# Two half-chunks of the shared expert done in the tail, one diagonal block per pair weighted by GpSimd, and a new instruction order

## The reference

```
xn  = layernorm(x)
q,k,v,gate = xn @ w_attn            # 16 query heads, 8 kv heads, head size 64
log_G = cumsum(log_sigmoid(6.9 + gate))
s   = rope(q) . rope(k) / 8
a   = exp(2*log|s| + log_G[t] - log_G[s] - max), causal       # = s^2 * decay, scaled
y   = (a @ v) / (sum(a) + 1e-6);  y = normalise(y) * ln_w
x1  = y @ w_proj
h   = layernorm(xn)*g + b
routed = top-2 of 7 experts, capacity 366 tokens, silu(h@W1)*(h@W3) @ W2, gated
shared = silu(h @ W1s) * (h @ W3s) @ W2s
out = x + x1 + routed + shared
```

## Time and profile before

| what | value |
|---|---|
| runs of the kernel before | 1078.84, 1072.55, 1076.85 us (median 1076.85) |
| profiled execution: its own time | 1071.44 us |
| profiled execution: span from first to last instruction | 1069.7 us |
| mean granted TensorE clock | 0.953 of full speed |
| PE busy | 941.8 us (88%) |
| DVE busy | 810.0 us (76%) |
| ACT busy | 682.6 us (64%) |
| POOL busy | 600.6 us (56%) |

### The profile page before, as it was taken

The page is one execution under the profiler, slowest core; times in us unless marked ns, Lnnn a source line. Parts: engine busy times, 40 slices in busy tenths (PEclk is TensorE's granted clock), DMA queues, the critical chain, the costliest instruction groups (busy, mean ns, idle before and its releaser), DMA issues.

```text
span 1069.7 us, 22031 instructions
## 1 busy us (share of the span) xinstructions
PE 941.8 (88%) x8487; PEld 661.7 (62%) x8487; DVE 810.0 (76%) x1503; ACT 682.6 (64%) x1141; POOL 600.6 (56%) x520
## 2 busy tenths in 40 slices
PE   4999989979898989999897989898998989898962
PEld 2675566656565756566665666665766666666642
DVE  5678648878888897778795868688777879686962
ACT  2343458767576767677586677677667768678730
POOL 0311429677767787655565574747366556556441
PEclk9999999999999999989998989899998999999985
DMA  9301213252525252614434342634252443434137
GB/s 264 88 1 45 55 47 90 64 114 49 125 50 124 48 124 73 133 46 99 109 72 97 76 99 67 142 68 107 72 132 55 102 107 77 103 80 94 42 56 197
DMA packets 92792, 96.00 MB, mean 90 GB/s; under 512 B 26605, under 2 KB 77677, under 8 KB 92560
## 3 DMA queue, kind: packets, MB, share of 16 engines
q1 hardware_dynamic: 87616, 91.92, 36.3%
q0 software_dynamic: 5072, 2.67, 1.8%
HBM read 49.47 MB, written 14.50 MB: 60 GB/s over the span
## 4 chain that ended last, share of the span: by engine, by line
PE 49%; DMA 17%; ACT 11%; DVE 9%; SPq 8%; issue 3%; POOL 1%; POOLq 0%; ACTq 0%; DVEq 0%
PE PS L570 15%; PE PS L748 12%; PE PS L778 9%; DMA Kt<-Kt 7%; DMA U<-H_d 6%; ACT U L924 6%; SPq L448 3%; SPq L499 3%; PE PS L613 2%; PE PS L616 2%; PE PS L623 2%; DMA SQ<-R_d 2%; ACT U L850 2%; ACT AX L924 1%; DVE PS L1349 1%
## 5 line engine op out<-in xcount | busy, mean ns | idle before, releaser
L748 PE MATMUL PS<-Qt,Kt 64*128 64x256 f32 (+1 forms) x2560 | 318.0, 394 | 64.7 <-DMA Kt<-Kt 36.6
L748 PEld LDWEIGHTS PS<-Qt,Kt 64*128 64x128 f32 x2560 | 251.3, 204 | 124.2 <-issue 36.8
L924 ACT ACTIVATE U<-PS,ESG,ES 128x512 f32<-128x512 f32 x288 | 206.7, 790 | 128.0 <-PE PS L748 116.7
L778 PE MATMUL PS<-U 128*64 128x256 f32 (+1 forms) x1920 | 202.2, 358 | 8.2 <-POOL U L1473 4.5
L778 PEld LDWEIGHTS PS<-U 128*64 128x64 f32 x1920 | 133.2, 137 | 77.9 <-issue 9.6
L1462 POOL TENSOR_TENSOR U<-U,consts 128x512 f32<-128x512 f32 x96 | 124.4, 1296 | 91.0 <-DMA U<-U 90.3
L1343 DVE TENSOR_TENSOR PS<-U 128x512 f32<-128x512 f32 x64 | 74.6, 1165 | 66.6 <-POOL U L1473 56.6
L1479 POOL TENSOR_SCALAR_AFFINE_SELECT U<-U 128x256 f32<-128x256 f32 x128 | 53.4, 420 | 113.2 <-ACT U L850 112.6
L1473 POOL TENSOR_TENSOR U<-U 128x768 f32<-128x768 f32 x41 | 76.2, 1858 | 61.6 <-ACT U L913 61.5
L1523 POOL TENSOR_TENSOR U<-U,SQ 128x1024 f32<-128x1024 f32 x32 | 77.8, 2430 | 54.6 <-DMA SQ<-R_d 54.6
L1349 DVE TENSOR_TENSOR PS<-U,PS 128x512 f32<-128x512 f32 x144 | 99.8, 693 | 7.6
(11 more groups left out here) (181 smaller groups left out, 1456.7 us busy)
## 6 DMA issues: line engine op xcount, KB each, us to landing
U<-U SPq DMA_DIRECT2D x192, 128.0 KB
U<-H_d SPq DMA_DIRECT2D x32, 512.0 KB
SQ<-R_d SPq DMA_DIRECT2D x64, 256.0 KB, 7.3
Kt<-Kt SPq DMA_DIRECT2D x32, 256.0 KB
U<-in_w SPq DMA_DIRECT2D x21, 256.0 KB, 4.8
acc<-in_x SPq DMA_DIRECT2D x4, 512.0 KB, 5.4
ye_d<-SQ SPq DMA_DIRECT2D x4, 512.0 KB, 7.4
R_d<-U SPq DMA_DIRECT2D x16, 128.0 KB
```

What stands on the lines that cost most here:

```text
L748: mm = te.matmul(bank[:, 256 * n:256 * n + 256 - lo], Kt[u % 2][(ki + hd) % 2][rows, 128 * j:128 * j + 128], Qt[p % 2][m // 2][rows, 256 * ...
L778: mm = te.matmul(P[4][64 * hd:64 * hd + 64, c + lo:c + 256], vt, A[s % NA][:, o:o + 256 - lo], start=begins and n == 0, stop=ends and n == 1)
L924: sq = s.activation(A[n % NA].rearrange("p (a n t) -> p n a t", a=2, n=2)[:, t], PS[:, first:first + 1024].rearrange("p (a n t) -> p n a t ...
```

## The change

`NTAIL = 2`: of the 8 halves of the shared expert `NSH = 6` stay in the opening. Halves 6 and 7 are transposed and used by the router there as before, but their `h` is kept in its own place (`HX`), and their up steps (`sup`, 16 single products), silu, product, down (`sdn`) and addition are new jobs of pair 31. Their weights are loaded once more (`sload`, three DMAs of 256 KB) into tiles of the raw queries, after the last swap. `HEAVY` is (3,) for all pairs, so in 23 pairs VectorE weights the w=1 block. All order tables have new numbers. ScalarE's off-diagonal squares wait for both scalings of ES (v_es 2 in place of 1). The work area grows by 256 columns.

```diff
+NTAIL = 2
+NSH = 8 - NTAIL
-HEAVY = [(3,)] * 9 + [(1, 3)] * 23
+HEAVY = [(3,)] * 32
...
-PE_FIRST: ("up", 33.04, 24.16, 6.2, 8, 4), ("down", 66.9, 24.8, 6.12, 8, 2)
+PE_FIRST: ('up', 33.34, 24.43, 6.57, 6, 4), ('down', 68.18, 25.67, 3.14, 6, 2)
-ACT_FIRST: ("silu", 39.95, 23.79, 6.11, 8, 4), ("es", 169, ...), ("e1", 172.32, ...), ("q", 190.18, 4, ...)
+ACT_FIRST: ('silu', 42.27, 24.01, 5.66, 6, 4), ('es', 181.22, ...), ('e1', 184.04, ...), ('q', 174.79, 1.88, ...)
-POOL_FIRST: ("scatter", 170.28, 4.09, 0, EARLY, 1), ("select", 294.1, 6.18, 0, 2, 1), ("q", 232.63, 8.35, 0, 2, 1)
+POOL_FIRST: ('scatter', 228.56, 15.63, 0, 6, 1), ('select', 263.31, 3.96, 10.48, 2, 1), ('q', 228.76, 11.76, 12.28, 2, 1)
...
+PE_AT: (19.99, 'sup', 0), (20.54, 'sup', 1), ... (28.15, 'sup', 8), (30.4, 'sup', 9), ... (41.42, 'sup', 15), (39.13, 'sdn', 0), (51.12, 'sdn', 1)
+ACT_AT: (19.39, 'sup', 0), (24.8, 'sup', 1), (25.33, 'sup', 2), (31.2, 'sup', 3), ... (64.65, 'sup', 7)
-ACT_AT: (35.85, 'sq', 0), (28.66, 'sq', 1), (62.53, 'down', 0), (15.77, 'square', 5)
+ACT_AT: (36.29, 'sq', 0), (30.5, 'sq', 1), (60.94, 'down', 0), (17.71, 'square', 5)
-POOL_AT: (9.49, 'heavy', 3), (69.16, 'norm', 0), (55.0, 'norm', 1)
+POOL_AT: (8.43, 'heavy', 3), (69.05, 'norm', 0), (61.0, 'norm', 1)
-SP_AT: (26.0, 'tops', 0), (33.34, 'rows', 0), (34.86, 'roots', 0), (36.65, 'spread', 0)
+SP_AT: (-11.68, 'sload', 0), (4.85, 'tops', 0), (26.83, 'rows', 0), (36.3, 'roots', 0), (37.69, 'spread', 0)
...
+                elif kind == "sload":
+                    sp.wait_ge(s_sq, 64 * 32)
+                    sp.wait_ge(g_q, 64)
+                    sy.dma_start(TW[0], w1s).then_inc(s_tw, 16)
...
-                ac.wait_ge(p_sd, 8)
-                ac.wait_ge(p_cb, 32)
+                ac.wait_ge(p_sd, NSH)
+                ac.wait_ge(p_cb, 4 * NSH)
...
@@ TensorE @@
+                elif kind == "sup":
+                    c, n = divmod(job[2], 8)
+                    f, w = divmod(n, 2)
+                    pb = bank_of(job)
+                    pe.wait_ge(s_tw, 48)
+                    te.matmul(pb[:, :], TW[w][:, 128 * f:128 * f + 128], HX[c], start=True, stop=True).then_inc(p_su, 1)
@@ TensorE @@
+                elif kind == "sdn":
+                    for q in range(4):
+                        for f in range(4):
+                            pe.wait_ge(v_su, 4 * c + f + 1)
+                            mm = te.matmul(pb[:, 128 * q:128 * q + 128], TG[c][f][:, 128 * q:128 * q + 128],
+                                           TW[2][:, 128 * f:128 * f + 128], start=f == 0, stop=f == 3)
...
@@ ScalarE @@
+                elif kind == "sup":
+                    s.activation(TG[c][f], P[BANK["sup", 31, 8 * c + 2 * f]][:, :], ACT.Silu).then_inc(a_su, 1)
...
@@ VectorE @@
+                elif kind == "sup":
+                    v.tensor_tensor(TG[c][f], TG[c][f], P[BANK["sup", 31, 8 * c + 2 * f + 1]][:, :], ALU.mult).then_inc(v_su, 1)
@@ VectorE @@
+                elif kind == "sdn":
+                    v.tensor_tensor(acc[:, o:o + 512], P[BANK[job]][:, :], acc[:, o:o + 512], ALU.add).then_inc(v_add, 1)
```

More of the change, by code:

```diff
@@ L55 @@
[L55 to L58, removed]
@@ new lines @@
+POOL_FIRST = [('norm', 79.34, 39.6, 7.36, 3, 1), ('scatter', 228.56, 15.63, 0, 6, 1), ('select', 263.31, 3.96, 10.48, 2, 1), ('k', 165.65, 16.94, 4.66, 2, 1), ('q', 228.76, 11.76, 12.28, 2, 1)]
+PE_AT = [(19.99, 'sup', 0), (20.54, 'sup', 1), (20.7, 'sup', 2), (20.8, 'sup', 3), (20.9, 'sup', 4), (21.0, 'sup', 5), (21.1, 'sup', 6), (21.81, 'sup', 7), (28.15, 'sup', 8), (30.4, 'sup', 9), (30.5, 'sup', 10), (30.95, 'sup', 11), (31.64, 'sup', 12), (31.69, 'sup', 13), (34.43, 'sup', 14), (41.42, 'sup', 15), (39.13, 'sdn', 0), (51.12, 'sdn', 1), (35.76, 'ss', 0), (68.82, 'wp', 0), (68.9, 'wp', 1), (3.61, 'xe', 0), (10.73, 'up', 0), (14.29, 'up', 1), (17.1, 'up', 2), (34.37, 'up', 3), (38.24, 'up', 4), (39.12, 'up', 5), (45.06, 'up', 6), (48.07, 'up', 7), (50.63, 'down', 0), (-26.21, 'k', 0), (-26.07, 'k', 1), (-18.13, 'q', 0), (-17.97, 'q', 1), (-13.58, 'v', 0), (6.96, 'v', 1)]
@@ L64 @@
 SP_FIRST = [("row", 0), ("swapk", 0), ("swapq", 0), ("keys", 0)]
-SP_AT = [(26.0, 'tops', 0), (33.34, 'rows', 0), (-26.51, 'swapk', 0), (-25.12, 'swapq', 0), (-21.73, 'keys', 0), (-21.74, 'row', 0), (-10.42, 'weights', 0), (-6.32, 'weights', 1), (34.86, 'roots', 0), (36.65, 'spread', 0)]
+SP_AT = [(-11.68, 'sload', 0), (4.85, 'tops', 0), (26.83, 'rows', 0), (-32.78, 'swapk', 0), (-23.64, 'swapq', 0), (-21.41, 'keys', 0), (-22.29, 'row', 0), (-21.4, 'weights', 0), (-11.64, 'weights', 1), (36.3, 'roots', 0), (37.69, 'spread', 0)]
 LOAD_AT = [20 * EXPERT_PAIRS[-1] + 76 + b for b in range(B)]
@@ L122, in wanted @@
         return p % 2 == i
+    if kind in ("sload", "sup", "sdn"):
+        return p == 31
     if kind in ("xe", "up", "down", "weights", "combine"):
@@ L254, in block_program @@
         SWPk = take(1024)
-        take = carve(6912)
+        take = carve(7168)
         Vt = [take(1024) for _ in range(2)]
@@ L261, in block_program @@
         ZT, RT, RR, MF = (take(256) for _ in range(4))
-        take = carve(20224)
+        take = carve(20480)
         HR = take(1024)
-        EXPERTS = 21248
+        EXPERTS = 21504
         take = carve(EXPERTS)
@@ L273, in block_program @@
         HL = sb("HL", 1)
+        HX = [U[:, 6144 + 512 * i:6656 + 512 * i] for i in range(NTAIL)]
+        TW = [U[:, 512 * i:512 * i + 512] for i in range(3)]
+        TG = [[RAWk[:, 0:512], RAWk[:, 512:1024], SWPk[:, 0:512], SWPk[:, 512:1024]],
+              [Kt[0][i][:, 512 * j:512 * j + 512] for i in range(2) for j in range(2)]]
         take = carve(3072)
@@ L286, in block_program, with hidden @@
         wv_ = take(512)
+        def hidden(half):
+            return HX[half - NSH] if half >= NSH else hT[:, 512 * half:512 * half + 512]
         hn_v = hn.rearrange("p (k c) -> p k c", c=HS)
@@ L348, in read_out @@
                 return v_wp, 2 * i + job[2] + 1
+            if kind == "sup":
+                n = job[2]
+                return (a_su, n // 2 + 1) if n % 2 == 0 else (v_su, n // 2 + 1)
+            if kind == "sdn":
+                return v_add, NSH + job[2] + 1
             if kind == "xe":
@@ L1121, in forget @@
                 v.tensor_scalar(ESG[:, :], ES[:, :], GUARD, None, ALU.mult).then_inc(v_es, 1)
-                chain(v.tensor_scalar(ES[:, :], ES[:, :], 0.125, None, ALU.mult))
+                v.tensor_scalar(ES[:, :], ES[:, :], 0.125, None, ALU.mult).then_inc(v_es, 1)
                 yield
```

77 lines of the change are left out of this document (49 added, 28 removed), and 7 rows, old and new, of tables (ACT_FIRST, PE_FIRST).

## The result

| | before | after |
|---|---|---|
| median of the runs | 1074.7 us (1068.89 to 1078.84, 4 runs) | 1044.33 us (1036.64 to 1050.26, 4 runs) |
| profiled execution: own time, span | 1071.44, 1069.7 us | 1044.84, 1043.0 us |
| mean granted TensorE clock | 0.953 | 0.982 |
| first scores | 142.30 | 126.66 |
| loop, first scores to the end of the last values | 884.8 us | 871.2 us |

The ratio is 0.972 (95% interval 0.964 to 0.980): 2.8% faster, some 30 us. I had forecast 1062, 15 us faster.

The account below looks back on a forecast made before the run. TensorE was taken to bound the opening and pair loop, a chain of small steps the tail. Start -18, loop 0, tail +3 made -15: 1056.4 profiled, 1062 us as median; range 1048 to 1074, likeliest case 1054 to 1069.

Parts of the forecast that it names:

- Part 1, the start: Opening: two shared-expert halves leave, scores start at 125.2, limited by GpSimd's query rotation; 18 us gained, between 11 and 25.
- the upper bound: First scores: ScalarE's exponential table load now lies before them; 1 us gained, bounds 0 and 2.3.
- Part 2, the loop: Pair loop: TensorE bounds it, so moved weighting and new order change nothing at the end; 0, with 8 us either way.
- my own sign: Failure test: first scores later than 131, or loop from first score to last value over 10 us from 885.
- HEAVY at zero: Loop: the w=1 block of 23 pairs goes from GpSimd to VectorE; 0 at the end, 2 us of slack for 1.
- The loop gains as well: Rival: a fifth of the loop's some 65 us of TensorE idle goes, 13 us, total 1049; chance 0.15.
- square behind sq: Rival: each odd pair's last ScalarE square comes late in 16 pairs, with a slower clock after; 1084 us; chance 0.1.
- Part 3, the tail: After the last values: added expert work delays the chain, partly won back; +3 us, bounds +0.5 and +11.
- The up products that I feared at the lower clock: Rival, tail: 8 ups cost 13.8 instead of 6.9 us and wp 6.3; 8 us more, total 1070; chance 0.2.
- the 2.5 us for less DMA beside it: Tail: new SP order issues loads earlier, so about 0.5 MB less competes with the spread; 2.5 us back.
- the 0.6 assumed: Tail: last wp gets 0.6 of 1.3 us back, with TensorE at work until a few us before.
- Carrying over: From profiled execution to median: the 5.4 us by which the shown runs' median exceeded it was added, 1056.4 to 1061.8.

Follow-up runs that it names:

- e11: The changed kernel with first queries rotated before all scatters, four VectorE operations before the routing wait, eight useless tail products: 1043.03 us, 0.970 of before.
- e4: The kernel before with three useless TensorE products ahead of the first score of each even pair from pair 2 on: 1061.82 us, ratio 0.987.
- e9: The kernel before with only ScalarE's sq of the even pair moved ahead of the odd pair's last off-diagonal square: 1068.24 us, ratio 0.995.
- e13: The kernel before with only HEAVY = (3,) in all pairs, so VectorE weights the w=1 block in 23 pairs: 1074.56 us, ratio 1.001.
- e8: The kernel before with GpSimd's new order list alone: 1075.69 us, ratio 1.002.

## Why the prediction was wrong in its size

In the profiled executions the change gave -26.6 us, where I had -15.

- **Part 1, the start: right in the sum, in part by luck.** First scores at 126.66 instead of 125.2, by the mechanism named (exponential, gk, one scatter, four rotation steps). The table load and ScalarE's decays, now ahead of the scores, gave 2.3 us by the fifth score, the upper bound, where I had taken 1. The two errors cancel: 17.9 gained, forecast 18. TensorE was not done at 119.7 but at 125.7, only 0.95 us ahead of the scores. I had not seen that the addition would hold its last `down` for 3.54 us, nor that the work behind that wait would be slow (4.80 us for what took 3.17 in e11). So TensorE was close to being the limit, which I had said it was not. Two readings were off as well: what held the up step for 1 us was VectorE's product, not ScalarE, and the exponential slipped by 2.3 us (117.70 against 115.42), not 1.2.
- **Part 2, the loop: this step failed.** I wrote "So 0 at the end" and, of the exchange of `sq` and square, "TensorE then waits 2 to 3.6 us for the key copy, which hides it. Zero". By my own sign (a loop over 10 us from 885) the forecast fails: it is 871.2. The 2.3 us above taken off, the loop gained 11.3 us. The hiding was right: idle time stayed at 79.5 to 79.8 us. I priced a wait at its length and took the products behind it as given: the term for TensorE's busy time in the loop, at 0, measured -13.9 us. The clock behind 12 of the 13 gaps was low, and the new lists made fewer and shorter gaps there; e4 shows the clock's part, e9 that the exchange of `sq` and square has a share. How the rest divides among the lists stays open. HEAVY at zero was right (e13).
- **The rival "The loop gains as well"** had the size (13 us) by luck, and the wrong place. Its "some 65 us of TensorE idle" are the waits ahead of score products alone (64.7); the loop's idle time was 79.5. It named VectorE's waits on GpSimd. Those fell with GpSimd's new order (8.2 us in e8), and e8 is no faster.
- **The rival "square behind sq"** had the place and the wrong sign. The waits at the value products came (9.9 and 7.9 us), the key copy's fell by 15.2, and "a slower clock after it" was the opposite of what happened.
- **Part 3, the tail: right in the sum**, +2.5 against +3, by errors that cancel. Counted from the last values, `ss` was 2.4 us late where my terms make 3.7 (4.4 less the 0.7 by which I had the values later), as the `wp` ahead of it took 3.71 us instead of 5.05. The up products that I feared at the lower clock kept it at the upper one: 1.00 from 998 to 1010, where before it was 0.50 between 1030 and 1032, behind an idle stretch of 3.26 us. The spread took 11.1 us, so the 2.5 us for less DMA beside it did not come. The last `wp` gave 0.7 for the 0.6 assumed.
- **Carrying over.** I added 5.4 us from the profiled execution to the median. After's median is 0.5 us below its profiled time, which makes 5.9 of the 17.7 us between 1062 and 1044.3.

The Trainium skill, TensorE: Matmul & The Clock Gate, "HAM oscillation — how this bites in real kernels", counts the loss of time at the lower level as half of that time. From before to after the 48 us fewer would be 24 by it, an estimate; TensorE's busy time fell by 13.9, 0.29 us for each. Counting only the low time in which TensorE was busy (some 63 and 22 us) it is 0.34. So the page names the mechanism that I missed, and the price here is smaller.

## What to carry to other kernels

Where TensorE bounds a loop and a stretch behind each long wait has a lower granted clock, price the wait as its length plus the slower work behind it. Look at the clock in pieces of 2 us around each repeated gap, not only at its mean. Several short waits in the same sum can be cheaper than one long one, so an edit that only moves idle time, or useless products in front of the semaphore, may gain. And a start that is made earlier has to be followed through the first pair: in e11 scatters ahead of selects took back nearly all of 4.1 us.

## What was unexpected of the hardware

Added work of 42.6 us made the kernel faster by 1.3% (e4). In after, four key-copy gaps of 1.7 to 2.7 us had a low stretch with them and five of 1.8 to 2.5 us had none, so the length of the gap alone does not say it. And an exchange of two instructions that makes TensorE's next input later shortened the kernel before by 0.5% (e9).
